# Four graph layers in one software pipeline: the blocks of all engines in another order, with other PSUM banks

## The reference, cut to what matters

```python
x = _layernorm(x + _L0_gnn_ref(x, adj, ...))   # layer 0: per head tanh(adj * (Xp C) Xp^T) @ Xp, 8 heads
x = _layernorm(x + _L1_gnn_ref(x, adj, ...))   # layer 1: hypergraph convolution, hidden width 512
x = _layernorm(x + _L2_gnn_ref(x, adj, ...))   # layer 2: attention by exp(leaky_relu(si + sj)), two hops
x = _layernorm(x + _L3_gnn_ref(x, adj, ...))   # layer 3: gated attention, scores = QK QK^T * adj
# inside layer 1
H = (adj != 0).astype(x.dtype)
Dn = jnp.einsum('nce,ne->nc', H, w)            # node degrees: the column that deg_m reads
Dn = jnp.where(Dn > 0, 1.0 / Dn, 0.0)
# inside layer 3
out = jnp.einsum('bnm,bmd->bnd', attn, xg)
out = out @ Wl.T + bl + xg @ Wr.T
```

## Time and profile before

| | |
|---|---|
| median of 3 runs | 1858.62 us (1857.68 to 1868.71) |
| the profiled execution | 1858.8 us |
| its span in the trace | 1857.0 us, mean granted TensorE clock 0.995 |
| PE busy | 1797.4 us (97%) |
| DVE busy | 1560.5 us (84%) |
| ACT busy | 1226.0 us (66%) |
| POOL busy | 878.0 us (47%) |

### The profile page before, as it was taken

The page is one execution under the profiler, slowest core; times in us unless marked ns, Lnnn a source line. Parts: engine busy times, 40 slices in busy tenths (PEclk is TensorE's granted clock), DMA queues, the critical chain, the costliest instruction groups (busy, mean ns, idle before and its releaser), DMA issues.

```text
span 1857.0 us, 42386 instructions
## 1 busy us (share of the span) xinstructions
PE 1797.4 (97%) x14472; PEld 1566.9 (84%) x14472; DVE 1560.5 (84%) x4444; ACT 1226.0 (66%) x2384; POOL 878.0 (47%) x1807
## 2 busy tenths in 40 slices
PE   5799999999999999999999999999999999999985
PEld 4688888888888888888888888888888888888874
DVE  5678888888888888888888888888888888888874
ACT  4566676676667666676667667667667667667653
POOL 1334544544544544544544454454454454454443
PEclk9999999999999999999999999999999999999998
DMA  4111212211211211211211211211111211211101
GB/s 153 38 41 58 64 32 64 64 34 62 64 37 60 63 42 54 63 42 55 64 46 50 64 50 47 64 50 47 63 50 47 64 49 47 64 50 46 41 29 34
DMA packets 99670, 100.00 MB, mean 54 GB/s; under 512 B 8320, under 2 KB 90368, under 8 KB 99200
## 3 DMA queue, kind: packets, MB, share of 16 engines
q1 hardware_dynamic: 99456, 97.29, 16.8%
HBM read 80.48 MB, written 16.78 MB: 52 GB/s over the span
## 4 chain that ended last, share of the span: by engine, by line
PE 93%; DVE 2%; ACT 1%; issue 1%; POOL 0%; DVEq 0%; ACTq 0%; POOLq 0%
PE psum L942 53%; PE psum L951 5%; PE psum L1021 4%; PE psum L1005 4%; PE psum L997 3%; PE psum L1083 3%; PE psum L1066 3%; PE psum L991 3%; PE psum L1158 3%; PE psum L1040 3%; PE psum L1151 3%; PE psum L962 3%; PE psum L1166 1%; PE psum L1104 1%; PE psum L1136 0%
## 5 line engine op out<-in xcount | busy, mean ns | idle before, releaser
L397 ACT ACTIVATE x<-res,shift,rstd 128x256 f32<-128x256 f32 x512 | 278.4, 594 | 69.4 <-DVE res L876 55.6
L383 POOL TENSOR_SCALAR edge_m<-edge_n 128x2 f32<-128x2 f32 x64 | 14.3, 223 | 476.1 <-DVE edge_n L825 476.1
L593 DVE BATCH_NORM_STATS2 stats<-res 128x6 f32<-128x256 f32 x512 | 191.9, 417 | 0.3
L942 PE MATMUL psum<-wk_hi,xT_hi 128*128 128x258 f32 (+1 forms) x512 | 185.9, 363 | 3.3 <-DVE xT_lo L588 3.3
L299 POOL TENSOR_TENSOR rstd<-var_eps,minus_half 128x2 f32<-128x2 f32 x256 | 178.8, 698 | 20.0
L608 DVE TENSOR_TENSOR masked<-psum,adjT 128x512 f32<-128x512 f32 x256 | 164.1, 684 | 22.9 <-PE psum L1005 22.8
L326 POOL TENSOR_TENSOR x_rest<-x,b_half 128x512 f32<-128x512 f32 x64 | 81.7, 1276 | 197.9 <-DVE res L638 197.9
L942 PE MATMUL psum<-wk_hi,xT_lo 128*128 128x258 f32 (+1 forms) x512 | 173.7, 339 | 0.0
L942 PE MATMUL psum<-wk_lo,xT_hi 128*128 128x258 f32 (+1 forms) x512 | 173.0, 338 | 0.0
L556 ACT ACTIVATE z<-hid_relu,hid_bias,hid_rstd 128x512 f32<-128x512 f32 x128 | 97.5, 809 | 96.6 <-POOL hid_bias L363 96.6
L942 PE MATMUL psum<-w_hi,zT_hi 128*128 128x256 f32 x512 | 144.4, 282 | 2.1 <-DVE zT_lo L588 1.1
(11 more groups left out here) (180 smaller groups left out, 6055.9 us busy)
## 6 DMA issues: line engine op xcount, KB each, us to landing
adjT<-in_adj_t SPq DMA_DIRECT2D x256, 128.0 KB, 2.5
xt_in<-in_xt SPq DMA_DIRECT2D x64, 256.0 KB, 2.9
x<-in_x SPq DMA_DIRECT2D x64, 256.0 KB, 2.7
out<-x SPq DMA_DIRECT2D x64, 256.0 KB, 2.6
wts<-in_adj SPq DMA_DIRECT2D x64, 128.0 KB, 2.3
wts<-in_w SPq DMA_DIRECT2D x1, 1028.0 KB, 7.6
wts<-in_w SPq DMA_DIRECT2D x1, 1024.0 KB, 11.8
wts<-in_w SPq DMA_DIRECT2D x1, 769.0 KB, 9.5
```

Source lines behind the costliest of these rows:

```text
L397: last = act.activation(xs[k + 1][:, g, :], res[k][:, g, :], ACT.Identity, scale=rstd[k][:, g:g + 1], bias=shift[k][:, g:g + 1])
L593: last = dve.bn_stats(stats[k][:, g, :], res[k][:, g, :])
L942: last = pe.matmul(dst, a, r, start=b == 0 and j == 0, stop=b == len(lhs) - 1 and j == 2)
```

## The change

All five `turn` functions are written in another order, some turn frames are shifted, and 23 of the 34 results in PSUM get another bank. No arithmetic is added or removed. The core of it:

```diff
-    ("rz_0", 3, 6, "rz_read_0"), ("rz_1", 0, 6, "rz_read_1"), ("hid_0", 4, 2, "hid_read_0"),
-    ("gram", 5, 6, "scores"), ("xT2", 7, 4, "xT2_lo"), ("hid_1", 6, 2, "hid_read_1"),
...
+    ("rz_0", 3, 6, "rz_read_0"), ("rz_1", 6, 6, "rz_read_1"), ("hid_0", 5, 2, "hid_read_0"),
+    ("gram", 3, 6, "scores"), ("xT2", 0, 4, "xT2_lo"), ("hid_1", 2, 2, "hid_read_1"), ("mix_0", 5, 6, "mix_read_0"),
+    ("headsT", 3, 1, "headsT_read"), ("mix_1", 4, 6, "mix_read_1"), ("y0_0", 7, 4, "y0_read_0"),
+    ("y0_1", 6, 4, "y0_read_1"), ("xp", 2, 0, "xp_read"), ("y12_0", 0, 4, "y12_read_0"), ("heads", 3, 1, "res0"),
+    ("xpT", 2, 0, "xpT_read"), ("zT_0", 6, 2, "zT_lo_0"), ("zT_1", 4, 2, "zT_lo_1"), ("y12_1", 5, 4, "y12_read_1"),
+    ("si", 3, 4, "e_both"), ("y1_0", 7, 2, "y1_read_0"), ("y1_1", 4, 2, "y1_read_1"), ("xcT", 3, 0, "xcT_read"),
+    ("conv", 7, 2, "res1"), ("prop", 1, 1, "node_r"), ("att_0", 6, 0, "masked_0"), ("att_1", 0, 0, "masked_1"),
...
 # DVE, before: after hop2 and res2 of the same turn
-                if on[1]:
-                    wait(dve, "prop", n[1])
-                    dve.tensor_scalar(deg_m[:, :].unsqueeze(2), degrees(), 1.2e-38, None, ALU.max) \
-                        .then_inc(sem("deg_inv_0"), 1)
...
 # DVE, after: between inc and edge_n, ahead of the masks
+                if on[0]:
+                    wait(dve, "prop", p[0])
+                    wait(dve, "adj1_loaded", n[0], 16)
+                    dve.tensor_scalar(inc[:, :, :], adjT[1][:, :, :], 0.0, None, ALU.not_equal).then_inc(sem("inc"), 1)
+                if on[1]:
+                    wait(dve, "prop_read", n[1])
+                    dve.tensor_scalar(deg_m[:, :].unsqueeze(2), degrees(), 1.2e-38, None, ALU.max) \
+                        .then_inc(sem("deg_inv_0"), 1)
+                if on[0]:
+                    wait(dve, "inc", n[0])
+                    dve.tensor_reduce(edge_n[:, :], inc[:, :, :], AX.X, ALU.add).then_inc(sem("edge_n"), 1)
...
 # ACT, after: rz_0 is read ahead of the normalisation of layer 1, the second tanh behind rz_1
+                    wait(act, "rz_0", n[6])
+                    act.activation(rz3[:, 0, 0:2 * D], ps("rz_0"), ACT.Copy).then_inc(sem("rz_read_0"), 1)
+                if on[4]:
+                    wait(act, "xT2", p[4])
+                    wait(act, "res2", p[4])
+                    normalise(1, n[4])
```

More of the change, by code:

```diff
@@ L261, in turn @@
                     sp.dma_start(vec1[:, :], v1.partition_broadcast(P)).then_inc(sem("w_1"), 16)
[L262 to L273, removed]
+                if on[7]:
+                    wait(sp, "x4", n[7])
+                    sp.dma_start(pair_at(out, (t.i - 7) * (G * P * D)), xs[4][:, :, :]).then_inc(sem("stored"), 16)
                 if on[0]:
@@ L473, in turn @@
                     last.then_inc(sem("qk_tanh"), 1)
[L474 to L477, removed]
+                    wait(act, "mix_1", p[6])
+                    wait(act, "mix_read_1", p[6])
+                    wait(act, "rz_0", n[6])
+                    act.activation(rz3[:, 0, 0:2 * D], ps("rz_0"), ACT.Copy).then_inc(sem("rz_read_0"), 1)
                 if on[4]:
@@ L641, in turn @@
                     last.then_inc(sem("res1"), 1)
+                if on[1]:
+                    if t.first(1):
+                        dve.wait_ge(sem("consts"), 1)
+                    wait(dve, "prop", p[1])
+                    wait(dve, "adj1_loaded", n[1], 16)
+                    dve.tensor_tensor(inc_b[:, :, P:P + 1], adjT[1][:, :, 0:1], ones[:, 0:G].unsqueeze(2), ALU.mult) \
+                        .then_inc(sem("edge_w"), 1)
                 if on[2]:
@@ L648, in turn @@
                         .then_inc(sem("node_r"), 1)
-                    if t.first(2):
-                        dve.wait_ge(sem("w_1"), 32)
-                    wait(dve, "node_r", n[2])
-                    hidden(0, n[2], p[2])
+                if on[5]:
+                    aggregate(2, n[5], p[5])
                 if on[6]:
@@ L659, in turn @@
                         .then_inc(sem("scores"), 1)
+                if on[2]:
+                    if t.first(2):
+                        dve.wait_ge(sem("w_1"), 32)
+                    wait(dve, "node_r", n[2])
+                    hidden(0, n[2], p[2])
                 if on[4]:
@@ L763, in turn @@
                 if on[1]:
-                    wait(dve, "prop", p[1])
-                    wait(dve, "edge_1", n[1])
-                    for g in range(G):
-                        last = dve.tensor_scalar(inc_b[:, g, 0:P], inc[:, g, :], edge_r[:, g:g + 1], None, ALU.mult)
-                    last.then_inc(sem("inc_b"), 1)
+                    layer_stats(0, n[1])
                 if on[2]:
@@ L1093, in turn @@
                     y0_of(1, t)
-                if on[6]:
-                    if t.first(6):
-                        pe.wait_ge(sem("consts"), 1)
-                    mix_of(0, t, n[6])
-                if on[1]:
-                    wait(pe, "headsT_read", n[1])
-                    claim("heads", t)
-                    for g in range(G):
-                        for c in range(NC):
-                            at = g * D + c * P
-                            last = pe.transpose(ps("heads")[:, at:at + P], headsT[:, c, g, :], ident[:, :])
-                    last.then_inc(sem("heads"), 1)
-                if on[6]:
-                    mix_of(1, t, n[6])
                 if on[0]:
@@ L1124, in turn @@
                     y12_of(0, t)
+                if on[1]:
+                    wait(pe, "headsT_read", n[1])
+                    claim("heads", t)
+                    for g in range(G):
+                        for c in range(NC):
+                            at = g * D + c * P
+                            last = pe.transpose(ps("heads")[:, at:at + P], headsT[:, c, g, :], ident[:, :])
+                    last.then_inc(sem("heads"), 1)
                 if on[0]:
```

479 lines of the change are left out of this document (242 added, 237 removed), and 7 rows, old and new, of the table TENANTS.

## The result

The changed kernel takes **1910.76 us** (median of 4 runs, 1907.36 to 1912.26), where the kernel before took 1861.39 us in the same comparison (4 runs, 1857.68 to 1868.71). The profiled execution took 1910.21 us, its span is 1908.4 us, which is 51.4 us more than the 1857.0 of before.

What follows compares the result with a forecast made beforehand. PE, busy throughout the steady turns, was taken as the bound, with the masks already on its edge. 1858.8 + 52 (58 turns of 0.90) + 2 for filling = 1912.8, with a little gain from Step 2 1911 us; range 1886 to 1930.

Steps and rivals of the forecast that it cites:

- Step 1: On DVE, deg_m ahead of the masks waits for ACT's copy of prop; masks and PE's pxT 0.90 us later each turn.
- The further 0.15 us for `xg_lo`: DVE's xg_lo and PE's qkT arrive almost together, so up to 0.15 us more a turn was possible; 0.90 was taken.
- the filling: Half dozen turns in which the pipeline fills: masks 0.41 us later, some 2 us in all.
- Step 2: On PE, mix_0 and mix_1 ahead of y0, heads behind y12_0: taken at nothing, range 0 to -32 us.
- Step 3: DVE's xp behind PE's xp, zT_lo_0 later with 0.2 us of cover left: taken at nothing, up to +17 us.
- Step 4: Banks, DMA order, POOL order: nothing; loads early enough, adj_n with 1 us to spare; weights while filling 0, 4 us either side.
- The better middle of the turn: Rival: no stall at the masks, gain from headsT on, 11 to 17 us, so 1843 us; chance of gain 0.07.
- the change that does nothing: Rival: deg_m's wait on DVE is covered and nothing else moves, 1859 us; chance 0.05.
- The turn that grows by more than the masks: Rival: zT_lo_0, xg_lo or a bank also comes late, 0.3 us a turn, 1928 us; chance 0.12.
- the rival of the falling clock: Rival: PE's clock falls in the stalls to a mean of 0.91, 160 us more, about 2070 us; chance 0.02.

Runs made afterwards that it cites:

- both repairs: Changed kernel with deg_m back behind the second hop's reads and ACT's copies of y12_1 and prop ahead of norm0 and xT0_hi: 1861.63 us, ratio 1.0.
- the first repair: Changed kernel with only deg_m put back behind the second hop's reads on DVE: 1860.39 us, ratio 0.999 to the kernel before.
- the two single repairs: Changed kernel with deg_m put back (1860.39 us), and, separately, with ACT's copies of y12_1 and prop ahead of norm0 and xT0_hi (1861.3 us).

## Why the prediction was right, point by point

**What bounds the kernel.** "The masks are already on the edge of PE's path" held in both directions: later masks cost (four kernels), and earlier masks gave 0.20 us a turn in one kernel and 27.76 - 27.57 = 0.19 us in the other.

**Step 1, `deg_m` ahead of the masks.** Mechanism, place and sign are shown by the pair of single edits (1860.39 with it undone, 1909.16 with it alone). Its terms were:

| term | forecast, us | measured, us |
|---|---|---|
| ACT's copy of `prop` ends, against the old start of the masks | 0.36 | 933.87 - 931.01 - 2.49 = 0.37 |
| ACT to DVE | 0.10 | 933.90 - 933.87 = 0.03 |
| `deg_m`, start to start | 0.11 | 933.97 - 933.90 = 0.07 |
| `edge_n`, start to start | 0.33 | 934.30 - 933.97 = 0.33 |
| sum | 0.90 | 0.80 |

The first and the last, read from the same instructions, were right. The handshake was taken from an exponential that feeds another DVE instruction, and the price of `deg_m` from a place where something else stood behind it. Both were too large, by 0.11 us together. The further 0.15 us for `xg_lo` didn't come: it ended at 935.65 + 0.66 = 936.31, `qkT` went at 936.61. The prediction had moved `xg_lo` by the whole delay of the masks and 0.2 us for the aggregate; but DVE had stood idle for 0.36 us before it, and that took up part of both. It starts 935.65 - 934.30 = 1.35 us behind the masks now, where it started 906.79 - 905.14 = 1.65 us behind them before.

**The sum.** Forecast were 58 x 0.90 = 52 us and 2 us in the filling. Measured were 3 + 53 = 56 turns of 0.80, 44.7 us, and 6.7 us in the filling, 51.4 in all. So the median, 1910.76 for 1911, agrees better than its parts: **the turn was sized 0.10 us too long, and the filling 5 us too short.** The steady part was forecast 7 us too dear, the filling 5 us too cheap, and 2 us were taken off for a gain of part 2 that didn't come. The mechanism was right; that the median came within 1 us is luck. What made the filling longer is only partly settled. The first 60 us of the changed kernel's profile had a clock of 0.89, those of the kernel before 1.00; but the kernel with both repairs had 0.89 as well and came to the same `pxT` at 218.15 us, 4.9 us later than the kernel before with the same turn. The twelve runs of the first repair show what lies between executions of one kernel: three with a mean granted clock of 0.994 took 1855.0 to 1856.5 us, nine with 0.988 to 0.991 took 1859.0 to 1862.5 us, about 5 us more. The profile of before had 0.995, and all four runs of the changed kernel had 0.987 to 0.990. So most of the 6.7 us can be such a difference, by this estimate; how many are the change's stays open.

**Step 2, mixes and heads.** Taken at nothing, with up to 32 us as the other end: it is nothing. Its two waits, L1088 and L963, stand at 17.3 and 10.3 us in 52 turns, for 19.3 and 10.7 in 54, 0.02 us a turn less at most; and the first repair, which keeps this step, is at 0.999.

**Step 3, `xp` and `zT_lo_0`.** Taken at nothing, rightly. DVE's idle time ahead of `xp` is 44.0 / 45 = 0.98 us where 1.5 was forecast. Of the cover, 0.2 us by forecast, a little more is left. DVE's `zT_lo_0` and PE's first of `y1_0`, answering to the earlier trace rows:

```profile
926.08 0.68 DVE L586 TENSOR_TENSOR zT_lo<-psum,zT_hi 128x512 fp32r<-128x512 f32 x1
...
927.08 0.28 PE L943 MATMUL psum<-w_hi,zT_hi 128*128 128x256 f32 x1
```

The one ends at 926.76, the other starts at 927.08 us: 0.32 us. DVE has a wait here that it didn't have before and that the prediction doesn't name: `aw_prod` (L910) waits for PE's second hop by 26.5 / 52 = 0.5 us a turn. It costs nothing either: the first repair has it too, 27.2 us in 54 turns.

**Step 4, banks and loads.** "`adj_n`, with 1 us to spare" was wrong: DVE's `deg` waits for this load in 23 turns, up to 1.7 us (18.1 us in all, in the list of waits above). It cost nothing, since DVE had its idle time ahead of `xp` to take it from, and the repaired kernel with the same order of loads is at 0.999.

**What would show it.** DVE idle before `deg_m` by 66.7 / 52 = 1.28 us (1.2 to 1.5 forecast), weight loads of `hop1_1` behind the masks by 1.03 us (0.8 to 1.1), a turn of 28.53 us (28.6).

**The rivals.** The better middle of the turn is refuted by the first repair, the change that does nothing by the result. The turn that grows by more than the masks is refuted by 0.80 and 0.80. The clock stayed at 1.00 from 200 to 1700 us with 0.62 us of idle PE a turn. The Trainium skill (TensorE: Matmul & The Clock Gate, "Why this matters for your kernels") warns of idle gaps that are longer than this one, so the rival of the falling clock read more into the page than it states, and the steady turns agree with the page.

That `deg_m` has to wait for ACT at all, though ACT only reads the bank as well, is the kernel's own wait on `prop_read`. The Trainium skill (PSUM — Partial Sum Buffer, "PSUM bank collisions raise a hardware error") states a rule that such a wait keeps: ACT and DVE may not access the same partitions of one bank at the same time, even if both only read. No run here shows a collision, and a kernel without that wait wasn't tried.

## What to carry to other kernels

Ask of each small instruction that moves in an in-order queue which wait comes with it and what stands behind it: here 0.07 us of work with a wait for ACT cost 0.80 us a turn and 2.6% of the time, because the two masks that stand behind it are what PE needs next. A wait was free here as long as a later wait of the same queue ended later anyway, so compare the ends, here ACT's copy (and the pieces of DVE behind it) against PE's `att_0`, and measure both from one common event. And where the profile shows a loop of engines, look for what starts it: moving PE's `att_0` ahead of `prop`, with DVE's and POOL's pieces out of its way, gave 0.5%, though PE had no idle time in the steady part of the profile; the waits of its weight loads showed what was to be had.

## What the runs showed of the hardware

**A DVE instruction of two elements a partition took 1.04 us.** In the changed kernel `inc_b` (L657) stands beside POOL's addition to `rz`. All engines at 943 us:

```profile
942.83 1.28 POOL L333 TENSOR_TENSOR rz<-rz,vec 128x512 f32<-128x512 f32 x1 [1.48 <-ACT rz L549]
943.08 1.04 DVE L657 TENSOR_TENSOR inc_b<-adjT,ones 128x2 f32<-128x2 f32 x1
```

They end together, POOL's at 944.11 and DVE's at 944.12. All 64 executions of that line (lowest, median and highest in ns), in the changed kernel and then in the kernel before:

```profile
L657 DVE TENSOR_TENSOR inc_b<-adjT,ones x64: 150/1040/1099, 22.1 to 1798.4; 128x2 f32<-128x2 f32 x64
```

```profile
L819 DVE TENSOR_TENSOR inc_b<-adjT,ones x64: 161/164/165, 18.8 to 1736.0; 128x2 f32<-128x2 f32 x64
```

A median of 1040 ns for 164: the new order put the instruction behind a POOL instruction that was under way, and it was held until that one ended. The first repair's profile has the same pair: POOL's ends at 910.83 + 1.28 = 912.11, and `inc_b`, which starts later behind it and takes only 0.91 us, ends at 911.21 + 0.91 = 912.12. The Trainium skill (SBUF — State Buffer, "SBUF: two separate sides") describes this: a port pair of SBUF that VectorE, with two inputs in SBUF, and GpSimd hold for a whole instruction, the second one waiting. The trace agrees. It costs DVE 0.9 us a turn. It costs the kernel nothing that the runs show: the first repair has it too and is at 0.999. In a kernel bound by DVE it would be 58 x 0.9 = 52 us, an estimate by the same arithmetic.

**The granted clock isn't the same from one execution to the next.** Over a whole execution it was 0.988 to 0.994 in the twelve runs of one kernel, the first repair, with the times above. The profiles, one of each kernel, show it in the filling: in the first 60 us it was between 0.89 and 1.00, and in two kernels with nearly the same turn the same `pxT` came 8 us apart, while from 200 to 1700 us it was 1.00 in all. A comparison of first turns in two single profiles can't tell an effect of some us; the period of the steady turns lay between 27.73 and 27.76 us in the kernel before, the two single repairs and the two together.
